# One float32 matmul per product in place of three float32r matmuls, in the feed-forward and the output mix of a transformer layer

## What is computed

```python
x = x + ln(attn(ln(x)))          # attention over channels, 16 heads of 16 channels
x = x + ln(ffn(ln(x)))
# attn: qk = x @ Wqk, v = x @ Wv; softmax over 16x16 channel distances; w = attn @ v; w @ Wo
# ffn:
h = layernorm(x, ln_g, ln_b)
logits = h @ Wr                   # 7 experts, top 2, capacity 732 tokens per expert
ye = (silu(xe @ W1[e]) * (xe @ W3[e])) @ W2[e]       # 256 -> 1024 -> 256, xe: gathered tokens
shared = (silu(h @ W1s) * (h @ W3s)) @ W2s           # for all tokens
out = routed + shared
```

## Time and profile before

| what | value |
|---|---|
| time, median of 3 runs | 1208.86 us (1207.46 to 1210.71) |
| the profiled execution's own time | 1209.31 us |
| its span, first to last instruction | 1207.5 us |
| PE busy, weight loads busy | 1092.5 us, 995.6 us |
| DVE, ACT, POOL busy | 678.9, 518.0, 385.0 us |
| mean granted TensorE clock | 0.958 of full speed |

### The profile page before, as it was taken

How to read it: one execution, slowest core, us unless ns; L and a number is a source line. 1 busy time by engine, 2 the same in 40 slices (tenths; PEclk the granted TensorE clock), 3 DMA queues, 4 the chain that set the end, 5 groups by cost and what they waited for, 6 DMA issues and landing times. The chain is left out here.

```text
span 1207.5 us, 20373 instructions
## 1 busy us (share of the span) xinstructions
PE 1092.5 (90%) x6744; PEld 995.6 (82%) x6744; DVE 678.9 (56%) x1727; ACT 518.0 (43%) x913; POOL 385.0 (32%) x333
## 2 busy tenths in 40 slices
PE   3476999998999998999999996999999999999980
PEld 2365888887888887888888885999999999999870
DVE  5553784464784554684455651455463554645796
ACT  2322343344334343433434432445454454544564
POOL 3410454011344011245011355253353533312233
PEclk9866999999999999999999997999999999999995
DMA  4694333024223015233014525153251532336496
GB/s 148 213 346 141 106 101 128 1 71 159 101 97 119 19 53 175 94 102 123 19 53 157 175 89 178 30 138 91 68 142 25 138 83 75 77 81 193 158 344 237
DMA packets 85500, 146.30 MB, mean 121 GB/s; under 512 B 10516, under 2 KB 61848, under 8 KB 85408
## 3 DMA queue, kind: packets, MB, share of 16 engines
q1 hardware_dynamic: 69072, 117.69, 28.8%
q0 software_dynamic: 16336, 27.48, 9.0%
HBM read 76.34 MB, written 68.78 MB: 120 GB/s over the span
## 5 line engine op out<-in xcount | busy, mean ns | idle before, releaser
L1497 DVE TENSOR_TENSOR sb_act<-bank,sb_act 128x512 f32<-128x512 f32 (+2 forms) x240 | 148.8, 620 | 407.8 <-PE bank L1015 367.8
L1013 PE MATMUL bank<-sb_h_hi,sb_wup_lo 128*128 128x512 f32 (+2 forms) x960 | 356.1, 371 | 23.0 <-DVE sb_h_lo L1467 14.1
L1015 PE MATMUL bank<-sb_h_hi,sb_wup_hi 128*128 128x512 f32 (+2 forms) x960 | 353.2, 368 | 0.0
L1014 PE MATMUL bank<-sb_h_lo,sb_wup_hi 128*128 128x512 f32 (+2 forms) x960 | 352.9, 368 | 0.0
L935 ACT ACTIVATE sb_act<-bank 128x512 f32<-128x512 f32 (+2 forms) x240 | 130.0, 541 | 429.0 <-PE bank L1015 362.2
L1013 PE MATMUL bank<-sb_wdn_hi,sb_act_lo 128*128 128x256 f32 (+1 forms) x848 | 249.5, 294 | 9.8 <-DVE sb_act_lo L1473 9.4
L1015 PE MATMUL bank<-sb_wdn_hi,sb_act_hi 128*128 128x256 f32 (+1 forms) x848 | 239.4, 282 | 0.0
L1014 PE MATMUL bank<-sb_wdn_lo,sb_act_hi 128*128 128x256 f32 (+1 forms) x848 | 239.2, 282 | 0.0
L1013 PEld LDWEIGHTS bank<-sb_h_hi,sb_wup_lo 128*128 128x128 f32 x960 | 182.9, 191 | 42.3 <-issue 17.4
L1015 PEld LDWEIGHTS bank<-sb_h_hi,sb_wup_hi 128*128 128x128 f32 x960 | 182.8, 190 | 23.2
L1014 PEld LDWEIGHTS bank<-sb_h_lo,sb_wup_hi 128*128 128x128 f32 x960 | 183.3, 191 | 18.1
(11 more groups left out here) (180 smaller groups left out, 1338.8 us busy)
## 6 DMA issues: line engine op xcount, KB each, us to landing
sb_xin<-in_L_ffn_W_dram SPq DMA_DIRECT2D x28, 512.0 KB, 4.2
sent_scratch<-sb_act SPq DMA_DIRECT2D x8, 1548.0 KB, 20.6
sb_xin<-in_L_attn_x_dram SPq DMA_DIRECT2D x16, 512.0 KB, 4.8
sb_x<-in_L_attn_x_dram SPq DMA_DIRECT2D x16, 512.0 KB, 4.6
x_scratch<-sb_x SPq DMA_DIRECT2D x16, 512.0 KB, 4.0
hT_scratch<-sb_hr SPq DMA_DIRECT2D x16, 512.0 KB, 2.7
sb_hfull<-hT_scratch SPq DMA_DIRECT2D x16, 512.0 KB, 4.6
y_scratch<-sb_ysb SPq DMA_DIRECT2D x14, 512.0 KB, 3.6
```

The costliest lines, as they stand in the source:

```text
L1013: t_.matmul(o, a_lo, b_hi, start=start, stop=False, skip_group_check=True)
L1014: t_.matmul(o, a_hi, b_lo, start=False, stop=False, skip_group_check=True)
L1015: return t_.matmul(o, a_hi, b_hi, start=False, stop=stop, skip_group_check=True)
L1497: v.tensor_tensor(act[:, m % 2, 0:c.w], bank[(4 if c.wide and m % 2 else 0) + 1][:, 0:c.w], act[:, m % 2, 0:c.w], ALU.mult).then_inc(act_o ...
```

## The change

`three` becomes `full`, one matmul of float32 operands; the tiles of the high halves become float32 tiles, so that what ACT writes there is the whole value. The low halves are computed as before, and waited for as before, but no product reads them (those of the Gram product excepted, which stays a float32r product of two halves). Its tile `xx` moves from `wdn_hi[1]` to `wdn_lo[1]`, because it has to stay float32r. The instructions of DVE, ACT, POOL and the DMA queues are the same, in the same order, but for the names of these tiles; on PE each group of three matmuls is one, in the same place, and no step is moved.

```diff
-        wup_hi = [sb(f"wup_hi{s}", [P, 2, KC, F], F32R) for s in range(2)]
+        wup_hi = [sb(f"wup_hi{s}", [P, 2, KC, F]) for s in range(2)]
-        wdn_hi = [sb(f"wdn_hi{s}", [P, FM, D], F32R) for s in range(2)]
+        wdn_hi = [sb(f"wdn_hi{s}", [P, FM, D]) for s in range(2)]
...
-        xx = wdn_hi[1][:, :, :].rearrange("p m d -> p (m d)").rearrange("p (t h d) -> p t h d", h=2, d=D)
+        xx = wdn_lo[1][:, :, :].rearrange("p m d -> p (m d)").rearrange("p (t h d) -> p t h d", h=2, d=D)
...
-        h_hi = sb("h_hi", [P, 2, KC, GW], F32R)
+        h_hi = sb("h_hi", [P, 2, KC, GW])
-        act_hi = sb("act_hi", [P, 4, GW], F32R)
+        act_hi = sb("act_hi", [P, 4, GW])
-        m_hi = sb("m_hi", [P, KC, D], F32R)
+        m_hi = sb("m_hi", [P, KC, D])
...
-            def three(o, a_hi, a_lo, b_hi, b_lo, start, stop):
-
-                t_.matmul(o, a_lo, b_hi, start=start, stop=False, skip_group_check=True)
-                t_.matmul(o, a_hi, b_lo, start=False, stop=False, skip_group_check=True)
-                return t_.matmul(o, a_hi, b_hi, start=False, stop=stop, skip_group_check=True)
+            def full(o, a, b, start, stop):
+
+                return t_.matmul(o, a, b, start=start, stop=stop, skip_group_check=True)
...
-                        ins = three(o, xT_hi[:, k, cols], xT_lo[:, k, cols], m_hi[:, k, :], m_lo[:, k, :],
-                                    k == 0, k == KC - 1)
+                        ins = full(o, xT_hi[:, k, cols], m_hi[:, k, :], k == 0, k == KC - 1)
...
-                        ins = three(o, wh, wl, h_hi[:, c.slot, k, 0:c.w], h_lo[:, c.slot, k, 0:c.w],
-                                    k == 0, k == KC - 1)
+                        ins = full(o, wh, h_hi[:, c.slot, k, 0:c.w], k == 0, k == KC - 1)
...
-                    ins = three(bank[2 + t // 2][0:w, (t % 2) * D:(t % 2 + 1) * D],
-                                act_hi[:, m % 4, cols], act_lo[:, m % 4, cols],
-                                wdn_hi[c.wset][:, m, :], wdn_lo[c.wset][:, m, :],
-                                m == 0 and t % 2 == 0, m == FM - 1)
+                    ins = full(bank[2 + t // 2][0:w, (t % 2) * D:(t % 2 + 1) * D], act_hi[:, m % 4, cols],
+                               wdn_hi[c.wset][:, m, :], m == 0 and t % 2 == 0, m == FM - 1)
```

More of the change, by code:

```diff
@@ L1165, in up @@
                 back = 1 if c.wide and not (first_wide and m == 0) else 0
-                for which, freed, full in ((0, silu_ok, a_ps), (1, act_ok, b_ps)):
+                for which, freed, filled in ((0, silu_ok, a_ps), (1, act_ok, b_ps)):
                     o = bank[(4 if c.wide and m % 2 else 0) + which][:, 0:c.w]
@@ L1170, in up @@
                         wh = wup_hi[c.wset][:, which, k, m * P:(m + 1) * P]
-                        wl = wup_lo[c.wset][:, which, k, m * P:(m + 1) * P]
-                        ins = three(o, wh, wl, h_hi[:, c.slot, k, 0:c.w], h_lo[:, c.slot, k, 0:c.w],
-                                    k == 0, k == KC - 1)
-                    ins.then_inc(full, 1)
+                        ins = full(o, wh, h_hi[:, c.slot, k, 0:c.w], k == 0, k == KC - 1)
+                    ins.then_inc(filled, 1)
             def down(c, m):
```

## The result

| | time, median | range | ratio to before |
|---|---|---|---|
| before | 1209.25 us (4 runs) | 1207.46 to 1210.71 | |
| changed | 1392.77 us (4 runs) | 1388.74 to 1396.87 | 1.152, 95% interval 1.148 to 1.156 |

The change makes the kernel 15.2% slower. 1398 us was predicted, 1385 to 1429 as the range. The profiled execution took 1388.74 us with a span of 1387.0 us, which is 179.5 us more than before (1207.5). It lies 4 us under the median, so stage by stage the comparison is of one execution with one other.

The account below looks back on a forecast made before the run. PE was taken to bound the kernel from the first shared chunk to the last `down`. The terms, 104.2 + 6.9 + 76 + 12.2 + 3 - 7.1 - 1.3 - 4.7 = 189 us, on 1209.3 gave 1398 us, range 1385 to 1429.

Parts of the forecast that it names:

- terms 1 to 3: Growth by columns: shared chunks' `up` and `down` +104.2 us, `o_mix` there +6.9, routed experts +76.
- the first rival: In wide products: a wide float32 record costs the overhead of a float32r one, giving 1429 us; chance 0.15.
- Term 3: Routed chunks, 7 experts: 10.9 us more for each, +76 us, with no idle PE time to take any.
- Term 6: Behind the last shared chunk: the first gather's wait goes, -7.1 us, and the clock may not fall, -1.3.
- Term 4: Held chunks: PE grows past DVE's 4.46 us a step and becomes the bound, +12.2 us.
- Term 5: `o_mix` in the first stage, 32 products, about half the records at half clock: +3 us.
- Term 7: Small waits of PE, at batch ends for DVE, for silu and the like, are partly covered: -4.7 us.
- terms 1 and 2: The 14 shared chunks of the second stage: `up` and `down` +104.2 us, 12 `o_mix` +6.9.
- the covers don't come: Rival: POOL's sends move with PE's end and small waits stay, 13 us more, 1411 us; chance 0.12.
- the weight loads: Rival: weight loads, not columns, limit PE's products, so the kernel gets faster, about 921 us; chance 0.02.
- it does something else: Rival: a float32 tile is taken in one short pass on PE, under 921 us; chance 0.01.
- half the clock: Rival: PE's clock falls to the half level under long float32 streams, about 2500 us; chance 0.02.

Follow-up runs that it names:

- e8: The kernel before with only `o_mix` as one float32 product, the low part of x left out of it: 1217.63 us, ratio 1.0058.
- e2: The kernel before with only `down` changed to float32 products: 1258.29 us, ratio 1.041.
- e1: The changed kernel with `down` back in its old form of three float32r matmuls: 1336.83 us, ratio 1.106.
- e4: The changed kernel with each product of `down` cut into two of 128 columns: 1408.74 us, one run.
- e5: The kernel before with each product of `down` cut into two of 128 columns: 1458.22 us, one run.
- e6: The kernel before without the high x low matmul in `up` and `down`, two float32r matmuls a product remaining: 1071.12 us, one run.
- e3: The changed kernel without the work on the low halves that no product reads: 1388.66 us, ratio 1.148.

## Why the prediction was right, term by term

**Prices, terms 1 to 3.** The step that carried the forecast was to take the price of a float32 product from four small plain products in the trace, and to scale it by columns. It held at every width to 0.01 us, so the first rival, a wide record with float32r's overhead, is out: 0.429 us at 512 columns, not 0.447. Term 3 came to 74.4 for 76. Experts 2 to 7 grew by 10.8 us each, for 10.9; the first grew by 9.3, since part of term 6 lies in it.

**Term 6 was right for the wait, with its reason, and near for the clock.** The wait of 7.09 us went because PE ends later than POOL's chain (e8, e2). The sizes behind it were both too large, which was luck: from the last batch end's transposes (651.10 before, 739.18 now) PE got to the end of the last shared `down` 12.1 us later, not 14.9, and POOL to the first gather 1.4 us later, not 4 to 5. The clock did not stay up, it fell later. Timeline of PE in the changed kernel:

```profile
842.31 9.52 PE L1013 MATMUL bank<-sb_h_hi,sb_wup_hi 128*128 128x384 f32 x24 [2.63 <-issue]
```

The first routed `up` takes 9.35 us for 24 x 0.322 = 7.73, so half clock costs 1.6 us there (granted clock 0.84 over it). Before, it took 8.92 for 36 x 0.175 = 6.30, 2.6 us (0.69). That gives 1.0 us back for the 1.3 of the prediction, within the routed stage of the table.

**Term 4 was right.** DVE's statistics are now 1351.35 - 1346.19 = 5.16 us apart in place of 4.46, which is PE's m, and DVE waits 0.62 us for each. In the profile of the changed kernel, timeline of DVE:

```profile
1345.58 0.69 DVE L1490 TENSOR_TENSOR sb_act<-bank,sb_act 128x512 f32<-128x512 f32 x1 [0.62 <-PE bank L1013]
1346.19 1.40 DVE L1236 BATCH_NORM_STATS2 sb_st<-sb_hr 128x6 f32<-128x256 f32 x4
...
1351.35 1.39 DVE L1236 BATCH_NORM_STATS2 sb_st<-sb_early 128x6 f32<-128x256 f32 x4
```

**Term 5 was too large, and luck hid it in one execution:** +3 was predicted, -1.2 measured in the profiled one. `o_mix` of the first two groups took 7.17 us in the changed kernel (timeline of PE):

```profile
65.01 7.17 PE L1013 MATMUL bank<-sb_m_hi,sb_wup_hi 128*128 128x256 f32 x32 [1.41 <-DVE sb_m_lo L1329]
...
107.41 5.73 PE L1013 MATMUL bank<-sb_h_hi,sb_wup_hi 128*128 128x512 f32 x8 [10.90 <-DVE sb_h_lo L1460]
```

The same 32 records took 8.55 us in e8, which had the same `o_mix`, and there the first `up` came at 110.46, 1.8 us later than before. 32 records at full clock are 6.9 us, so in the one most ran at full and in the other a part at half clock. With no change to what precedes it, this `o_mix` starts at 65.01 here, 66.29 in e8 and 65.10 before. e1 and e4 run the first stage exactly as the changed kernel does, and their first `up` starts at 109.93 and 110.97. With the old `o_mix` it starts at 108.64 (before), 108.97 (e2), 107.75 (e5) and 107.49 (e6). So the same stage differs by up to 3.6 us between executions, and the means, 109.7 of four (107.41, 109.93, 110.97, 110.46) and 108.2 of four, differ by 1.5: the forecast's sign, half its size, and no more than the scatter allows to say. What stays open is what raises the clock earlier in the one than in the other; that a longer phase gets the higher clock sooner, on which the +3 leant, is not shown.

**Term 7 was too small, and it is the one real miss.** For the small waits -4.7 was taken. By columns the shared stage grows by 111.1 us (terms 1 and 2) and it grew by 101.4, so 9.7 were given back there. The largest place is the end of a batch, from its last transposes to the third `up` behind them. Windows of the kernel before, of the first two batch ends and of the rest of the second batch:

```profile
283.23:302.32 19.09, 13.53 (x75) 11.26 (x73) 7.42 (x27) 8.40 (x14) 2.78 (x2) 0.91 0.51 169
467.24:486.40 19.16, 13.51 (x75) 11.26 (x73) 7.42 (x27) 8.38 (x14) 2.79 (x2) 0.91 0.50 168
302.32:467.24 164.92, 164.48 (x1008) 144.94 (x1007) 101.59 (x272) 64.62 (x109) 46.83 (x42) 1.00 0.25 84
```

The same of the changed kernel:

```profile
312.97:331.11 18.14, 13.94 (x57) 8.63 (x56) 7.19 (x26) 8.14 (x13) 2.79 (x2) 1.00 0.55 177
525.48:544.82 19.34, 15.47 (x58) 9.12 (x56) 7.19 (x26) 8.25 (x13) 2.79 (x2) 0.91 0.51 166
331.11:525.48 194.37, 194.37 (x735) 126.24 (x733) 101.60 (x273) 65.16 (x109) 47.78 (x42) 1.00 0.22 71
```

Outside the batch end the second batch grows by 194.37 - 164.92 = 29.45 us; 30 m's at 0.93 and four `o_mix` at 0.57 make 30.2. In a batch end two m's should add 1.9 us. The first gets 0.95 shorter and the second 0.18 longer, so 2.8 and 1.7 us are given back, and 0.5 at the third, shorter one. I had counted only DVE's wait there (1.23 + 0.97 us before, 0.93 + 0.67 now). Before, PE also stood still for ACT's silu (0.77 us) and ran the `up` behind it in part at half clock: eight of its records are 0.427 us apart, and it takes 4.46 us for 2.79. The changed kernel has no such wait there; what makes its second batch end 1.2 us longer than its first is another `up`, in part at half clock (5.23 us for 3.53; granted clock 0.91 against 1.00).

The same pair stands once more in the first of the last two chunks, between the router's matmuls and the `down` behind the `up`. Timeline of PE, before:

```profile
685.65 1.85 PE L1122 MATMUL bank<-sb_wr,sb_hr 128*128 128x7 f32 x16
689.56 0.50 PE L1013 MATMUL bank<-sb_h_hi,sb_wup_lo 128*128 128x512 f32 x1 [2.07 <-ACT sb_act L935]
...
694.00 0.28 PE L1013 MATMUL bank<-sb_wdn_hi,sb_act_lo 128*128 128x256 f32 x1
```

And in the changed kernel:

```profile
778.44 1.85 PE L1119 MATMUL bank<-sb_wr,sb_hr 128*128 128x7 f32 x16
781.67 3.70 PE L1013 MATMUL bank<-sb_h_hi,sb_wup_hi 128*128 128x512 f32 x8 [1.39 <-ACT sb_act L935]
785.21 0.38 PE L1013 MATMUL bank<-sb_wdn_hi,sb_act_hi 128*128 128x256 f32 x1
```

This stretch takes 8.35 us before and 6.77 now, where an `up` should have added 0.6: 2.2 us given back, 0.7 by the shorter wait and the rest by the clock (4.44 us for 2.79 before, 3.54 for 3.43 now). So 5.0 of the 9.7 us lie at the three batch ends and 2.2 here. The other 2.5 are spread, 0.5 to 0.8 us in each of the three batches and 0.6 in the rest of the last two chunks, and were not taken apart.

**The chances.** All rivals are out: the wide record's overhead by the distance of 0.429; that the covers don't come, by the gather wait; the weight loads by e4 and by the routed stage; that it does something else, by the two records a product; half the clock, by 1.00 in the routed and the held stage, under 428 us in which PE had almost nothing but float32 products. The total came within 5 us of the forecast (1392.77 for 1398) by the right terms: what was off in terms 3, 5 and 7 (about 2, 4 and 5 us in the profiled execution) lies on the same side and did not cancel.

## What to carry to other kernels

Where one engine is late in every stage, price its instructions by the distance between starts of the same kind in the trace of before, even if the kind occurs only four times in a small product, and scale by columns; it was exact to 0.01 us here, where the busy share of the weight loads pointed the other way. Add to it the places where that engine still waits, with the clock it has behind each wait: they give back some of the loss when it gets slower. In e6, which made it faster, about half of the reckoned gain of 250 to 285 us did not come; waits and clock are the likely cause there, not a shown one. And before you remove work from the bound engine, look at how much slack the others have per step, not in total.

## What was not expected of the hardware

- A float32r record has a floor: 0.111 us from start to start at 128 columns with a weight load for each (e5), twice its columns; a float32 record of 7 columns stands 0.112 us from the next. Three float32r matmuls of 256 columns, at 0.119 each, already stand near it, and splitting them finer costs more than float32 does.
- A float32 product of 128 columns stands at 0.111 us for each of its two records, so at that width a float32 product costs 0.222 us and three float32r matmuls 0.333. The comparison that this case lost at 256 columns (0.430 against 0.357) would turn at 128 columns. The cut `down`s of e4 and e5 show it (1.33 / 6 us a float32 product of 128 columns, 2.63 / 8 for three float32r matmuls); no kernel here was built on it.
- The first float32r record behind float32 records reads 0.2 to 0.4 us early in the timeline, with no time lost over the whole m (e2, e1).
- A shorter wait can cost more than it saves when the clock falls behind the next one: without DVE's work on the low halves (e3, one execution) the batch ends became 2.4 and 1.1 us longer, with an `up` of 6.19 us for 3.43 in the first.
